# Probabilities turned whole from batch 2 on, the stack completed by transfers between SBUF rows, and other orders in the opening and in batch 0

## The chip, the cores and the metric

One core of a Trainium2 chip runs one program, a fused cross-attention and feed-forward layer over 16 batches. The metric is the device time of one execution in microseconds: 1970.97 us, the median of 3 runs (1969.54 to 1971.58).

## The reference, cut to what matters

```
x: (16, 512, 512)   ctx: (16, 77, 512)
n = layernorm(x)
Sim = n @ w1 + ctx @ w2 + (n * w3) @ ctx^T + b           # (512, 77) per batch
A = softmax(Sim over the 77)                              # "probabilities"
hq_hat = A @ ctx                                          # (512, 512)
hc_bar = softmax(max over 77 of Sim, over the 512 rows) @ n
x1 = x + [n, hq_hat, n * hq_hat, n * hc_bar] @ W_qv + b_qv
m = layernorm(x1)
h = m @ W1 + b1                                           # 2048 wide
act = relu(h + phase term of sin(theta + 0.1 h))
out = x1 + act @ W2 + b2
```

## The kernel before, in words

Every float32 product is made of three reduced-precision matmuls (`three`): each operand is split into a high part (a cast by ScalarE) and a low part (value minus high, a subtraction by VectorE), and high x high, high x low and low x high are summed in PSUM. A matmul has 128 x 128 stationary and 128 x 512 moving elements.

The context has 77 rows (J), so the products with the probabilities are packed instead (`stacked`): the high and low part of the turned probabilities and the parts of the context rows are stacked along the 128 rows that are summed, in two blocks of `at_s`. Block 0 holds the 77 rows of the high part and below them the first 51 rows (JA = 128 - 77) of the low part; block 1 holds 77 rows of the high part again and the 26 remaining rows of the low part, 103 rows in all (JB). So the turned probabilities are needed at SBUF rows other than those on which they come out of a plain turn. Compute engines keep their rows, so the kernel splits first and turns afterwards: `prob_high` (ScalarE, two copies) and `prob_low` (VectorE, two subtractions) lay out in `split_prob` what each block is to hold, `prob_turn` (TensorE) turns both blocks of each of 4 row tiles through PSUM, 8 turns, and `stack_out` (ScalarE) and `second_stack_out` (VectorE) copy the two blocks to `at_s`. `split_prob` lies in the buffer `prs`, which otherwise holds the split products n * hq_hat.

Each engine has its own written-out list of work, and semaphores join them. A stage f = 0 to 15 (FT = 16) of batch b makes one slice of 128 hidden columns: `hidden(b, f)` (12 matmuls to `hid`), on ScalarE phase and h, on VectorE the reduction of the phase, on ScalarE the sine, on VectorE the sine term, then relu and its two parts; `second(b, f)` (12 matmuls to `acc`) follows LAG = 3 stages later. In between stands the attention of the next batch, n = b + 1: the spreads (the two parts of the normalized, turned x, T) and g (the scaled context) at f = 0 to 2, `sim` at f = 3, `sim_rows` at 4, `spread_max` at 5, `prob_turn` at 8, the stack copies at 8 and 9, `hq_hat(n, 0)` at NA - 1 = 9, the attention products at NA = 10 and the second normalization at 11 to 14. SP loads x, the turned x and the context rows of the next batch (`ctx_load`) and stores the output; POOL streams the weights, whose split copies were written to DRAM during batch 0, and makes the square roots.

The opening (`attention_first` on each engine) makes ten chunks of context rows times W_qv (`rows_in`, `high_parts`, `low_part`, `multiply`, `product_add`, `product_out`), keeps them in DRAM (hqw), and does the attention of batch 0 between them. POOL issues the loads of w3, w0 and x of batch 1 there. In batch 0 (`first`) the weights are also split (`w1_high`, `w1_low`, `tile_high`, `tile_low`), which loads ScalarE and VectorE more than later batches do. `add_b2` adds the last bias to the residual, `add_first_part` and `add_last_part` add the two sums of `acc`.

## Time and profile before

| | |
|---|---|
| median of 3 runs | 1970.97 us |
| the profiled execution | 1970.5 us |
| its span in the trace | 1968.7 us |
| TensorE matmul busy | 1948.3 us, 99%, 8807 instructions |
| TensorE weight load busy | 1598.2 us, 81% |
| VectorE busy | 1387.2 us, 70% |
| ScalarE busy | 988.9 us, 50% |
| GpSimd busy | 389.4 us, 20% |
| DMA | 391.73 MB, mean 199 GB/s |

The span is the time between the first and the last instruction; the rest of the execution's time lies around it. Matmuls are pipelined, so a matmul that is shown with 390 ns follows the one before it after a shorter time; the spacing of their starts is what counts. The granted clock (PEclk) is TensorE's share of full speed, at one of two levels, 1.2 and 2.4 GHz; a value between is a mean over the stretch.

### The profile page before, as it was taken

Reading aid. Unit: us, or ns where it says so; the run is one execution under the profiler, and the core shown is the slowest. Engines: PE = TensorE matmul, PEld = TensorE weight load, DVE = VectorE, ACT = ScalarE, POOL = GpSimd, SP = SyncE. Lnnn points to the kernel's source line nnn. Section 1 sums busy time; section 2 is a strip of 40 time slices with the busy share of each in tenths; the row PEclk is TensorE's granted clock in tenths of the full one; section 3 lists DMA queues with packets and bytes.
Section 4 is the critical chain, followed back from the end, with each engine's and each line's share of the span. In section 5 each row is a group of like instructions: output and inputs, shape, how many; then the busy total and the mean of one; then the engine's idle time right before and its main releaser. Section 6 shows DMA issues by size and latency. Waiting matters only on the chain.

```text
span 1968.7 us, 24691 instructions
## 1 busy us (share of the span) xinstructions
PE 1948.3 (99%) x8807; PEld 1598.2 (81%) x8807; DVE 1387.2 (70%) x2405; ACT 988.9 (50%) x1676; POOL 389.4 (20%) x834
## 2 busy tenths in 40 slices
PE   8899999999999999999999999999999999999999
PEld 6678888888888888888888888888888888888887
DVE  6888776767777676776767767676776767767554
ACT  4574635536355363644636355363653636446343
POOL 1122212121211212112121211212112121121210
PEclk9999999999999999999999999999999999999999
DMA  8476947577474775747667485764747757476473
GB/s 247 166 266 240 291 145 224 182 212 222 152 224 144 243 220 160 237 145 222 203 189 226 138 236 166 225 221 155 232 134 242 222 166 231 146 221 181 146 216 119
DMA packets 140849, 391.73 MB, mean 199 GB/s; under 512 B 21876, under 2 KB 34856, under 8 KB 138808
## 3 DMA queue, kind: packets, MB, share of 16 engines
q0 software_dynamic: 83568, 304.29, 49.6%
q1 hardware_dynamic: 57016, 85.83, 14.0%
q8 instruction: 71, 1.16, 0.2%
q14 instruction: 50, 0.41, 0.1%
q10 hardware_dynamic: 144, 0.04, 0.0%
HBM read 351.83 MB, written 38.27 MB: 198 GB/s over the span
## 4 chain that ended last, share of the span: by engine, by line
PE 92%; DVE 3%; ACT 2%; DMA 1%; issue 1%; SPq 0%; DVEq 0%; ACTq 0%
PE acc L500 17%; PE acc L502 17%; PE acc L501 17%; PE hid L502 11%; PE hid L500 11%; PE hid L501 11%; PE mis L586 1%; PE acc L508 1%; PE acc L509 1%; PE mis L508 1%; PE mis L509 1%; PE mis L500 1%; PE mis L502 1%; PE mis L501 1%; DMA ph<-in_ctx_turned 1%
## 5 line engine op out<-in xcount | busy, mean ns | idle before, releaser
L500 PE MATMUL acc<-ws,act 128*128 128x512 f32 x1024 | 402.8, 393 | 1.7 <-DVE act L1174 1.7
L500 PE MATMUL hid<-T,w1s 128*128 128x512 f32 x1024 | 402.8, 393 | 0.4 <-ACT h L849 0.3
L502 PE MATMUL acc<-ws,act 128*128 128x512 f32 x1024 | 399.2, 390 | 0.0
L502 PE MATMUL hid<-T,w1s 128*128 128x512 f32 x1024 | 399.0, 390 | 0.0
L501 PE MATMUL acc<-ws,act 128*128 128x512 f32 x1024 | 398.7, 389 | 0.0
L501 PE MATMUL hid<-T,w1s 128*128 128x512 f32 x1024 | 398.7, 389 | 0.0
L1168 DVE TENSOR_SCALAR kk<-ph 128x512 f32<-128x512 f32 x256 | 108.8, 425 | 329.5 <-ACT ph L846 329.5
L855 ACT ACTIVATE act<-h 128x512 fp32r<-128x512 f32 x256 | 162.0, 633 | 351.7 <-DVE h L1160 330.3
L846 ACT ACTIVATE ph<-hid,hbias 128x512 f32<-128x512 f32 x256 | 175.8, 687 | 285.3 <-PE hid L502 285.0
L1509 POOL DMA_DIRECT2D ws<-w2x_dram x240 | 127.5, 532 | 556.2 <-PE acc L502 546.7
L1174 DVE SCALAR_TENSOR_TENSOR act<-h,act 128x512 fp32r<-128x512 f32 x256 | 176.0, 688 | 74.4 <-ACT act L855 73.1
L500 PEld LDWEIGHTS acc<-ws,act 128*128 128x128 f32 x1024 | 192.4, 188 | 41.7 <-DVE act L1174 2.5
L500 PEld LDWEIGHTS hid<-T,w1s 128*128 128x128 f32 x1024 | 192.3, 188 | 41.7 <-issue 1.2
L502 PEld LDWEIGHTS hid<-T,w1s 128*128 128x128 f32 x1024 | 192.2, 188 | 40.4
L502 PEld LDWEIGHTS acc<-ws,act 128*128 128x128 f32 x1024 | 192.2, 188 | 40.4
L501 PEld LDWEIGHTS acc<-ws,act 128*128 128x128 f32 x1024 | 192.4, 188 | 38.9
L501 PEld LDWEIGHTS hid<-T,w1s 128*128 128x128 f32 x1024 | 192.5, 188 | 38.7
L1503 POOL DMA_DIRECT2D w1s<-w1x_dram x240 | 129.6, 540 | 454.1 <-PE hid L502 442.1
L1160 DVE SCALAR_TENSOR_TENSOR h<-ph,camp,h 128x512 f32<-128x512 f32 x256 | 191.0, 746 | 0.0
L849 ACT ACTIVATE h<-hid,cols 128x512 f32<-128x512 f32 x256 | 174.6, 682 | 26.0 <-DVE act L1174 26.0
L1170 DVE TENSOR_TENSOR ph<-ph,kk 128x512 f32<-128x512 f32 x256 | 177.4, 693 | 8.8
L859 ACT ACTIVATE ph<-ph 128x512 f32<-128x512 f32 x256 | 158.3, 618 | 1.3 <-DVE ph L1170 1.0
(181 smaller groups left out, 2741.9 us busy)
## 6 DMA issues: line engine op xcount, KB each, us to landing
w1s<-w1x_dram POOLq DMA_DIRECT2D x240, 512.0 KB, 3.9
ws<-w2x_dram POOLq DMA_DIRECT2D x240, 512.0 KB, 4.6
ws<-wqx_dram POOLq DMA_DIRECT2D x56, 512.0 KB, 3.6
full<-in_x_turned SPq DMA_DIRECT2D x15, 1024.0 KB, 8.2
out_x<-X SPq DMA_DIRECT2D x15, 1024.0 KB, 4.7
X<-in_x SPq DMA_DIRECT2D x14, 1024.0 KB, 8.6
w_raw<-in_L_ffn_W SPq DMA_DIRECT2D x32, 256.0 KB, 3.8
w1x_dram<-w1s POOLq DMA_DIRECT2D x16, 512.0 KB, 4.0
```

The lines of the kernel that those rows point to most:

```text
L500: pe.matmul(dst, w_hi, m_hi, start=start, stop=False)
L501: pe.matmul(dst, w_hi, m_lo, start=False, stop=False)
L502: mm = pe.matmul(dst, w_lo, m_hi, start=False, stop=stop)
L846: nc.scalar.activation(ph[:, f % 2], hid[:, f % 2], ACT.Identity, bias=hbias[:, f:f + 1], scale=HSCALE).then_inc(t_done, 1)
L849: nc.scalar.activation(h2[:, f % 2], hid[:, f % 2], ACT.Identity, bias=b1c[:, f:f + 1], scale=1.0).then_inc(h2_done, 1)
L855: nc.scalar.activation(act[:, f % 4, 0], h2[:, f % 2], ACT.Relu).then_inc(act_hi, 1)
L859: nc.scalar.activation(ph[:, f % 2], ph[:, f % 2], ACT.Sin, scale=TWO_PI_BELOW).then_inc(s_done, 1)
L1160: ve.scalar_tensor_tensor(out=h2[:, f % 2], in0=ph[:, f % 2], scalar=camp[:, f:f + 1], in1=h2[:, f % 2], op0=ALU.mult, op1=ALU.add).then_i ...
L1170: ve.tensor_tensor(ph[:, f % 2], ph[:, f % 2], kk[:], ALU.subtract).then_inc(r_done, 1)
L1174: ve.scalar_tensor_tensor(out=act[:, f % 4, 1], in0=h2[:, f % 2], scalar=0.0, in1=act[:, f % 4, 0].bitcast(F32), op0=ALU.max, op1=ALU.subtract
L1503: po.dma_start(w1s[:, s].rearrange("p a c k -> p (a c k)"), w1x_dram[f % FT].rearrange("p a c k -> p (a c k)")).then_inc(w1_in[s], 16)
L1509: po.dma_start(ws[:, slot_of(p)], tile_source(p, last, w2x_dram, wqx_dram)).then_inc(w_in[slot_of(p)], 16)
```

## The change

From batch 2 on (n > 1), `whole_prob_turn` turns the unsplit probabilities at f = 6: four turns of 77 columns to rows 0 to 76 of one PSUM bank. `whole_stack_out` (ScalarE, f = 7) casts them to the high rows of block 0 and copies these to block 1. `whole_stack_low` (VectorE, f = 7) writes the low part to `at_lo`, rows 0 to 76 of a part of `prs`, and SP moves its first 51 rows to rows 77 to 127 of block 0 and the other 26 to rows 77 to 102 of block 1 (`stack_low_in`), two transfers between SBUF rows of 104 and 53 KB. `hq_hat(n, 0)` waits for them, and for `max_exponentials`, for which `prob_turn` waited before. Batches 0 and 1 keep the old way.

In the opening: `context_high(0, 0)`, `sim_bias(0)`, `row_exponentials(0)` and, on VectorE, `context_low(0, 0)`, `low_part(5)`, `low_part(6)` and `low_part(7)` change places; SP puts `product_out(2)` and `rows_in(8)` ahead of two weight loads; POOL's load of w3 waits for one low part fewer, that of w0 also for the high parts of chunk 6, and that of x for one low part more; ScalarE makes g of batch 1 at its end. In batch 0: the spreads and `g_low` of batch 1 stand at f = 0 and 1, and `add_b2` moves from f = 3 to 6 (one tile each) to f = 12 and 15 (two tiles each).

The diff, with few lines around each edit and indentation shortened:

```
@@ -133,6 +133,7 @@
...
 split_high = [split_prob[:, :, 2 * k * J:(2 * k + 1) * J] for k in range(2)]
+at_lo = prs[0:J, 1, 1]
 e_bc = sb("e_bc", [P, R])

@@ -205,7 +206,7 @@
...
 ebc_done = sem("ebc_done"); erec_done = sem("erec_done"); at_done = sem("at_done")
-split_hi = sem("split_hi"); split_lo = sem("split_lo"); at_out = sem("at_out")
+split_hi = sem("split_hi"); split_lo = sem("split_lo"); at_out = sem("at_out"); at_low = sem("at_low"); at_in = sem("at_in")
 hqh_done = sem("hqh_done"); full_done = sem("full_done")

@@ -392,6 +393,12 @@
...
         stack_load(n, hqw_raw, hqw_tail, hqw_dram, ctx_in)
+    def stack_low_in(n):
+        sp.wait_ge(at_low, n - 1)
+        sp.dma_start(at_s[J:P, 0].bitcast(F32), at_lo[0:JA].bitcast(F32)).then_inc(at_in, 16)
+        sp.dma_start(at_s[J:JB, 1].bitcast(F32), at_lo[JA:J].bitcast(F32)).then_inc(at_in, 16)

@@ -429,10 +436,10 @@
...
         rows_in(7)
+        product_out(2)
+        rows_in(8)
         first_tile_load(0)
         first_tile_load(1)
-        product_out(2)
-        rows_in(8)
         product_out(3)

@@ -471,6 +478,8 @@
...
                 continue
+            if f == NA - 3 and not first:
+                stack_low_in(n)
             if n + 1 == B:

@@ -622,6 +631,12 @@
...
+    def whole_prob_turn(n):
+        pe.wait_ge(prob_done, n + 1)
+        for t in range(RT):
+            tr = pe.transpose(mis[0:J, 1, t * P:(t + 1) * P], prob[:, t], ident[:])
+        tr.then_inc(at_done, 1)
     def prob_turn(n):

@@ -634,6 +649,9 @@
...
             pe.wait_ge(at_out, 2 * (n + 1))
+            if n > 1:
+                pe.wait_ge(ebc_done, n + 1)
+                pe.wait_ge(at_in, 32 * (n - 1))
             pe.wait_ge(hq_lo, 2 * (n + 1))

@@ -720,8 +738,10 @@
...
                 spread_max(n)
-            if f == 8 and not last:
+            if f == 8 and first:
                 prob_turn(n)
+            if f == 6 and not first and not last:
+                whole_prob_turn(n)
             if f == 3 and not last:

@@ -884,6 +904,13 @@
...
+    def whole_stack_out(n):
+        sc.wait_ge(at_done, n + 1)
+        need(sc, att_done, RT * n)
+        nc.scalar.copy(at_s[0:J, 0], mis[0:J, 1]).then_inc(at_out, 1)
+        sc.wait_ge(at_out, 2 * n + 1)
+        nc.scalar.copy(at_s[0:J, 1], at_s[0:J, 0].bitcast(F32)).then_inc(at_out, 1)
     def w0_high(n, c):

@@ -901,7 +928,6 @@
...
         g_high(0)
-        context_high(0, range(0, 1))
         high_parts(4)

@@ -910,10 +936,11 @@
...
             full_copy(0, t)
+        context_high(0, range(0, 1))
+        sim_bias(0)
         high_parts(6)
-        sim_bias(0)
+        row_exponentials(0)
         high_parts(7)
-        row_exponentials(0)
         prob_high(0)

@@ -946,20 +973,24 @@
...
         product_copy(9)
+        g_high(1)
...
             g = FT * b + f
-            if f == 1 and not last:
+            if f == 1 and not first and not last:
                 spread_high(n, 0, pn)
...
                 row_exponentials(n)
-            if f == 6 and not last:
+            if f == 6 and first:
                 prob_high(n)
+            if f == NA - 3 and not first and not last:
+                whole_stack_out(n)
+            if f == NA - 1 and first:
+                stack_out(n)
             if f == NA - 1 and not last:
-                stack_out(n)
                 w0_high(n, 0)

@@ -979,7 +1010,10 @@
...
                 continue
-            if f == 1:
+            if f == 0 and first:
+                for c in range(C):
+                    spread_high(n, c, pn)
+            if f == 1 and not first:
                 spread_high(n, 2, pn)

@@ -1214,6 +1248,10 @@
...
+    def whole_stack_low(n):
+        ve.wait_ge(at_out, 2 * n + 1)
+        low(at_lo, mis[0:J, 1], at_s[0:J, 0]).then_inc(at_low, 1)
     def second_stack_out(n):

@@ -1281,23 +1319,23 @@
...
     def add_b2(n, t):
-        ve.wait_ge(x2_done, RT * n + t + 1)
+        ve.wait_ge(x2_done if n else a_evac, RT * n + t + 1)
         if n == 0:
...
-        ve.wait_ge(xb2_done, RT * (b + 1))
+        need(ve, xb2_done if b else x2_done, RT * (b + 1))
         ve.wait_ge(ffn2_done, FT * b + NA - LAG)
...
-        if whole:
+        if whole or b == 0:
             ve.wait_ge(xb2_done, RT * (b + 1))
-        else:
+        if not whole:
             ve.wait_ge(ffn2_done, FT * (b + 1))

@@ -1320,7 +1358,6 @@
...
             norm_first(t)
-        context_low(0, range(0, 1))
         low_part(3)

@@ -1330,14 +1367,14 @@
...
         turned_low(0, 3, 0, full_done, t1_lo)
+        low_part(5)
         sim_column(0)
-        low_part(5)
         product_add(2)
+        context_low(0, range(0, 1))
         product_add(3)
-        low_part(6)
         product_add(4)
         row_max(0)
-        low_part(7)
+        low_part(6)
         probabilities(0)

@@ -1346,6 +1383,7 @@
...
         context_low(0, range(1, 2))
+        low_part(7)
         row_mean(0, range(2, C))

@@ -1393,7 +1431,7 @@
...
                 chunk_low(n, 0)
-            if f == 2 and not last:
+            if f == 2 and not first and not last:
                 g_low(n)

@@ -1406,8 +1444,10 @@
...
                 sine_term(g - 1, (f - 1) % FT)
-            if f == NA - 2 and not last:
+            if f == NA - 2 and first:
                 second_stack_out(n)
+            if f == NA - 3 and not first and not last:
+                whole_stack_low(n)
             if first and 3 <= f < 3 + CN - GAP:

@@ -1415,15 +1455,24 @@
...
                 scale(n, 1)
+            if f == 0 and first:
+                g_low(n)
+                spread_low(n, 0, pn)
+                spread_low(n, 1, pn)
             if f == 1 and not last:
                 sim_column(n)
-                spread_low(n, 0, pn)
-                spread_low(n, 1, pn)
+                if first:
+                    spread_low(n, 2, pn)
+                    spread_low(n, 3, pn)
+                else:
+                    spread_low(n, 0, pn)
+                    spread_low(n, 1, pn)
             if f == FT - 1 and n + 1 < B:
...
                 center(n + 1, 1)
-            if first and 3 <= f < 3 + RT:
-                add_b2(b, f - 3)
+            if first and f in (NA + 2, NA + 5):
+                for t in range(2 * (f - NA - 2) // 3, 2 * (f - NA - 2) // 3 + 2):
+                    add_b2(b, t)
             if not first and f in (3, 4):

@@ -1432,8 +1481,9 @@
...
                 probabilities(n)
+            if f == 6 and first:
+                prob_low(n)
             if f == 6 and not last:
-                prob_low(n)
                 row_mean_scale(n)

@@ -1575,11 +1625,12 @@
...
         po.wait_ge(s_w1q_lo, C)
-        po.wait_ge(c_tlo, 4)
+        po.wait_ge(c_tlo, 3)
         po.dma_start(w3_sb[:], wqv_dram[3]).then_inc(s_w3, 16)
         po.wait_ge(tr1, RT)
+        po.wait_ge(c_thi, GAP + 1)
         po.dma_start(w0_sb[:], wqv_dram[0]).then_inc(s_w0, 16)
-        po.wait_ge(c_tlo, GAP + 1)
+        po.wait_ge(c_tlo, GAP + 2)
         po.dma_start(X[:, 1], x_rows[1]).then_inc(x1_in, 16)
```

## Rows read from the trace of the kernel before

**Rows 1.** Windows: length, busy us by engine, granted clock, DMA share, GB/s

```profile
0.00:77.00 77.00, 67.76 (x299) 53.70 (x300) 57.34 (x123) 33.95 (x62) 12.28 (x28) 0.96 0.65 200
77.00:200.00 123.00, 115.31 (x507) 91.52 (x507) 99.56 (x173) 75.19 (x132) 27.34 (x55) 0.97 0.72 249
200.00:1840.00 1640.00, 1639.93 (x7444) 1349.39 (x7443) 1165.34 (x2006) 828.74 (x1398) 327.24 (x706) 1.00 0.64 197
```

**Rows 2.** TensorE's waits: tile, line, releaser; total us, times, longest

```profile
PE mis L500 <- DVE T L1027: 4.6, 1, 4.6
...
PE acc L500 <- DVE act L1027: 3.7, 2, 1.9
...
PE mis L615 <- ACT tmp_w L864: 1.9, 1, 1.9
```

**Rows 3.** Timeline of TensorE, `prob_turn`, one batch: start, duration, line, tiles, shapes

```profile
728.79 0.27 PE L630 MATMUL mis<-ident,prs 128*128 128x128 f32 x1
728.90 0.27 PE L631 MATMUL mis<-ident,prs 128*103 128x128 f32 x1
...
729.90 0.40 PE L501 MATMUL acc<-ws,act 128*128 128x512 f32 x1
```

**Rows 4.** Timeline of TensorE, `spread_max` of the same batch

```profile
712.00 0.60 PE L622 MATMUL mis<-ident,rmax 128*128 128x128 f32 x4
...
712.67 0.39 PE L501 MATMUL acc<-ws,act 128*128 128x512 f32 x1
```

**Rows 5.** Timeline of TensorE, `sim_rows` of the same batch

```profile
706.22 0.43 PE L615 MATMUL mis<-ident,tmp_w 77*128 77x77 f32 x4
...
706.76 0.39 PE L501 MATMUL acc<-ws,act 128*128 128x512 f32 x1
```

**Rows 6.** Timeline of VectorE, f = 5 and 7 of the same batch

```profile
715.96 0.48 DVE L1203 TENSOR_TENSOR prob<-prob,rrec 128x308 f32<-128x308 f32 x1
...
726.86 0.75 DVE L1160 SCALAR_TENSOR_TENSOR h<-ph,camp,h 128x512 f32<-128x512 f32 x1
```

**Rows 7.** Timeline of TensorE, `second` at f=6, `hq_hat(n, 0)` at f=9

```profile
717.91 0.39 PE L500 MATMUL acc<-ws,act 128*128 128x512 f32 x1
...
737.85 0.39 PE L508 MATMUL mis<-at_s,hqs 128*128 128x512 f32 x1
```

**Rows 8.** Timeline of ScalarE, f = 6 and 7 of the same batch

```profile
719.34 0.44 ACT L879 CAST prs<-prob 128x308 fp32r<-128x308 f32 x1
...
725.08 0.67 ACT L846 ACTIVATE ph<-hid,hbias 128x512 f32<-128x512 f32 x1
```

**Rows 9.** DMA issues: count, KB each, median us from issue to landing

```profile
bqv_bc<-in_L_xattn_b_qv SPq DMA_DIRECT2D x1, 256.0 KB, 6.9
...
tmp_w<-in_ctx_turned SPq DMA_DIRECT2D x16, 154.0 KB, 6.4
```

**Rows 10.** Short windows of the opening and of batch 0, columns of rows 1

```profile
18.00:20.00 2.00, 0.27 (x2) 0.25 (x2) 1.60 (x3) 1.98 (x5) 0.00 (x0) 1.00 0.17 54
...
32.00:34.00 2.00, 1.86 (x7) 1.61 (x8) 1.79 (x4) 0.09 (x1) 1.30 (x2) 0.56 1.09 369
...
82.00:83.00 1.00, 1.00 (x6) 0.84 (x5) 0.97 (x2) 0.86 (x2) 0.00 (x0) 1.00 0.68 268
```

**Rows 11.** Timeline of TensorE, similarity of batch 1 in batch 0

```profile
95.44 0.68 PE L500 MATMUL mis<-T,gs 128*77 128x512 f32 x1 [4.62 <-DVE T L1027]
...
100.57 0.40 PE L500 MATMUL acc<-ws,act 128*128 128x512 f32 x1
```

**Rows 12.** Chain that ended last, in order: start, us, what

```profile
24.59 10.70 DMA ph<-in_ctx_turned
```

**Rows 13.** Timelines of ScalarE and VectorE in batch 0

```profile
91.63 1.48 ACT L813 ACTIVATE tmp_w<-tmp_w,cols 128x77 f32<-128x77 f32 x4
...
94.01 1.28 DVE L1027 TENSOR_TENSOR T<-full,T 128x512 fp32r<-128x512 f32 x2
...
126.62 0.68 DVE L1287 TENSOR_TENSOR X<-X,b_bc 128x512 f32<-128x512 f32 x1
```

More of the change, by code:

```diff
@@ L473, in body @@
                         continue
+                    if f == NA - 3 and not first:
+                        stack_low_in(n)
                     if n + 1 == B:
@@ L623, in spread_max, with whole_prob_turn @@
                 tr.then_inc(mbc_done, 1)
+            def whole_prob_turn(n):
+                pe.wait_ge(prob_done, n + 1)
+                for t in range(RT):
+                    tr = pe.transpose(mis[0:J, 1, t * P:(t + 1) * P], prob[:, t], ident[:])
+                tr.then_inc(at_done, 1)
             def prob_turn(n):
@@ L722, in body @@
                         spread_max(n)
-                    if f == 8 and not last:
+                    if f == 8 and first:
                         prob_turn(n)
+                    if f == 6 and not first and not last:
+                        whole_prob_turn(n)
                     if f == 3 and not last:
@@ L953, in body @@
                     g = FT * b + f
-                    if f == 1 and not last:
+                    if f == 1 and not first and not last:
                         spread_high(n, 0, pn)
@@ L981, in body @@
                         continue
-                    if f == 1:
+                    if f == 0 and first:
+                        for c in range(C):
+                            spread_high(n, c, pn)
+                    if f == 1 and not first:
                         spread_high(n, 2, pn)
@@ L1395, in body @@
                         chunk_low(n, 0)
-                    if f == 2 and not last:
+                    if f == 2 and not first and not last:
                         g_low(n)
@@ L1408, in body @@
                         sine_term(g - 1, (f - 1) % FT)
-                    if f == NA - 2 and not last:
+                    if f == NA - 2 and first:
                         second_stack_out(n)
+                    if f == NA - 3 and not first and not last:
+                        whole_stack_low(n)
                     if first and 3 <= f < 3 + CN - GAP:
@@ L1424, in body @@
                         center(n + 1, 1)
-                    if first and 3 <= f < 3 + RT:
-                        add_b2(b, f - 3)
+                    if first and f in (NA + 2, NA + 5):
+                        for t in range(2 * (f - NA - 2) // 3, 2 * (f - NA - 2) // 3 + 2):
+                            add_b2(b, t)
                     if not first and f in (3, 4):
@@ L1434, in body @@
                         probabilities(n)
+                    if f == 6 and first:
+                        prob_low(n)
                     if f == 6 and not last:
-                        prob_low(n)
                         row_mean_scale(n)
```

70 lines of the change are left out of this document (50 added, 20 removed).

## The prediction

> **What bounds the kernel now.** I read first how busy each engine is in four stretches, then what TensorE waited for. From 200 to 1840 us, which is most of batches 1 to 15, TensorE is busy in 1639.93 of 1640.00 us at full granted clock, while VectorE and ScalarE have 29% and 49% to spare [rows 1]. There the time is the number of TensorE instructions times their spacing, and work taken from any other engine is worth nothing. The opening (0 to 77 us) has 9.2 us without TensorE work and batch 0 (77 to 200) has 7.7 us; the granted clock is 0.96 and 0.97 in them [rows 1], so part of their matmuls ran at the lower of the two levels. The list of TensorE's waits names where: 4.6 us once, for the low half of T before the similarity of batch 1; twice at the split context rows, the longest 1.9; 1.9 once before `sim_rows` of batch 0 [rows 2]. So there are three accounts: the steady batches, the opening, batch 0.
>
> **Account 1, the steady batches: eight turns become four.** Spacing is read from start to start. `prob_turn` begins at 728.79 and the second matmul behind it starts at 729.90 [rows 3]: 1.11 us. One matmul is in that; 23 of them start from 706.76 to 712.00 us [rows 4, 5], 0.228 us each. So eight turns take 0.88 us. `spread_max` is four turns of 128x128: 712.00 to 712.67, less one spacing, 0.44 us [rows 4]. `whole_prob_turn` issues four turns whose stationary block has 77 columns and whose moving block is the same 128x128 identity, so I price it like `spread_max`, 0.44 us. Bounds: 0.31 us, what the four 77-wide turns of `sim_rows` took by the same subtraction [rows 5], and 0.88 if nothing is won. It applies to batches 2 to 15, fourteen of them: 14 x 0.44 = 6.2 us, bounds 0 and 8.0.
>
> A rule bears on this price. The row shows that in `prob_turn` the turn with 103 stationary columns follows 0.11 us behind that with 128, and 0.88 for eight says that both take that [rows 3]; four turns with 128 stationary and 77 moving columns took only 0.31 [rows 5]. The Trainium skill, page "TensorE: Matmul & The Clock Gate", section LDWEIGHTS, says that a weight load costs its columns divided by 1.2 GHz; by that rule `sim_rows` would have been the dearer one and 77 stationary columns the cheap case. The trace goes with the moving columns, so the sum keeps 0.44; the other reading is rival 3.
>
> **Does the new stack arrive in time?** Three new waits stand on TensorE's path.
> First, `whole_prob_turn` moves from f = 8 to f = 6 and now waits for the probabilities themselves. In the batch read, VectorE finished them at 716.44, and hidden(6) gave way to the next matmuls at 717.91 [rows 6, 7]: 1.5 us to spare. A turn that waited longer than 0.44 us would eat the gain of its batch. `row_exponentials` and `probabilities` keep their places, so I cost this at nothing.
> Second, ScalarE. Its two copies of `prob_high` (0.44 and 0.45 us, from 719.34 to 720.03) go from f = 6; two copies of 77 x 512, about 0.6 us each, come at f = 7 ahead of phase(7), which started at 725.08 [rows 8]; one copy goes at f = 9. Phase(7) comes about 0.6 us later. VectorE loses the two short subtractions of `prob_low` and trades a copy of 103 x 512 for a subtraction of 77 x 512, one f earlier. Queued behind on both engines are h, relu and the low half of act; TensorE takes these three f later, and neither of its engines was late once in this stretch [rows 1, 2]. Nothing.
> Third, the DMAs. VectorE's sine term of f = 7 ended at 727.6 [rows 6]; 0.6 later by ScalarE and 0.7 for the subtraction gives 728.9. SP has nothing in its queue there (its x load of f = 6 is long out) and needs 1 us to issue two transfers. `hq_hat(n, 0)` comes at 737.85 - 0.44 = 737.4 [rows 7], 7.5 us behind the second issue. The load of the same size on SP's queue, 154 KB, took 6.4 us from issue to landing in the median of 16 [rows 9], with six others behind it; here two go alone. At 6.4 us it still fits, with 1.1 to spare. The Trainium skill, page "DMA: Bandwidth & Descriptors", in its section on the anatomy of one DMA, gives about 2.0 us fixed plus bytes at 436 GB/s, an estimate of 2.4 us for this one; no run here shows such a transfer yet. The waits for ebc_done and at_in add no instruction of the array. Account 1 stays at 6.2.
>
> **Account 2, the opening.** `sim_bias(0)` leaves its place behind `high_parts(6)`, which waited for a context load; with it go TensorE's wait of 1.9 us [rows 2] and what followed: the clock was granted at 0.56 in 32 to 34 us [rows 10], the lower level for most of it, and six matmuls ran at 0.43 us instead of 0.228, the spacing of 12 matmuls in 5.13 us that batch 0 shows [rows 11], another 1.2. Together 3.1 us. Of the 9.2 us there remain, without those 1.9 and about 3.4 of the start (some 1.5 until the identity is there, and the longer of the two waits for context rows), some 3.9: a wait of 1.8 at chunk 3 [rows 2], and smaller ones up to `hq_hat(0, 0)`. The one of 1.8 goes, since `low_part(3)` no longer stands behind `context_low`; but the turns that follow need VectorE's `turned_low`, which now stands behind `product_add(0)` and so behind the b_qv row. That landed 6.9 us after its issue [rows 9], just ahead of this addition. w3's 1 MB is now issued one context chunk sooner, into transfers that are still at work; before, it came behind an interval (18 to 20 us) with a DMA share of 0.17 [rows 10]. That fills the hole, and may hold b_qv up by 1 to 2 us. Later it pays: w3 and w0 no longer sit ahead of rows 6, 7 and the hqw stack (row load 7 took 10.7 us, and the chain that ended last ran through it [rows 12]), and `high_parts(7)` and `low_part(7)` leave the road to `hq_hat(0, 0)` in part. Of these 3.9 I count 0.4. From `hq_hat(0, 0)` to the end of the opening TensorE has no gap, but VectorE hasn't either, and `low_part(7)` now falls into that stretch (0.6 us); I count it as hidden, its cover being the 2 us between chunk products and their use. Account 2: 3.5 us; bounds 1 and 6.
>
> **Account 3, batch 0.** At f = 3 the similarity of batch 1 started at 95.44 after 4.62 us of nothing, and its 12 matmuls took until 100.57 [rows 11], 2.4 us more than at full clock. What it waited for was VectorE's low half of T, chunks 2 and 3, at 94.01, behind ScalarE's `g_high`, 1.48 us for four scalings and 0.45 for the cast, from 91.63 [rows 13]. The change takes `g_high(1)` ahead of the batch and does the four spreads one f sooner. Without it VectorE could have gone on 2.4 us earlier. Against that: ahead of the batch `g_high(1)` needs the context load, and the DMA engines were still 68% busy at 82 to 83 us [rows 10], so it will wait until near 82 and push phase(0) back by some 1.7 us (1.9 for itself, less what ScalarE had free there); and four spreads in a row put phase(1), and with it hidden(3), back by some 1.5. TensorE's one long wait becomes two or three short ones. I take 1.9 us for the earlier start, plus the 2.4 of the clock: 4.3. The clock's 0.97 over 123 us [rows 1] is 3.7 us at full level, which the 5.13 us of these matmuls and the wait ahead of them use up; so the other 3.1 us of waits in this batch, all short ones, left it at the upper level, and I expect the same of the new ones. Bounds: 0 (the new waits add up to the old one, and the clock falls all the same) and 7.0.
> `add_b2` leaves f = 3 to 6. Only the one of f = 6, 0.68 us at 126.62 [rows 13], stands in a stretch where VectorE runs without a gap and TensorE waits for act: 0.6 us gained. At f = 12 and 15 VectorE has room; nothing lost. Some of this is eaten by ScalarE's table loads at f = 5 and 6, which nothing moves. Account 3: 4.5 us, bounds 0 and 7.6.
>
> **Sum.** 6.2 + 3.5 + 4.5 = 14.2 us. The profiled execution took 1970.5 us (its span 1968.7 and 1.8 around it), 0.5 below the median of the runs. 1970.5 - 14.2 = 1956.3; against the median 1956.8. I predict 1956.5 us.
>
> **Rivals.**
> 1. Only the steady part comes. The opening is held by b_qv and batch 0 by the late context load, at 1 and 0 to 1.5 us: 1970.97 - 6.2 - 1 to 2.5, that is 1961.3 to 1963.8. For it: both new orders stand on transfers in a loaded stretch. Against: 1.9 us at `sim_rows` was a pure matter of order.
> 2. The transfers come late, and the kernel is slower. Place: `hq_hat(n, 0)` of batches 2 to 15. Every microsecond past 7.5 from the second issue costs 14 us. With 10.7 us, the longest of these loads [rows 12], the wait is 3.2 us in each batch, 45 us in all, less 14: 2002. It decides from a landing of 7.5 + 14.2/14 = 8.5 us. Against: that load had the saturated DMA of the opening.
> 3. The turns go by their stationary columns: 0.11 x 77/128 = 0.066 us each, 0.26 for four, 0.62 saved per batch, 8.7 in all: 1954.0. That is what the LDWEIGHTS rule of the Trainium skill would make of it. Rows 3 and 5 speak against.
> 4. The stack is not ready at f = 6: a wait of 0.4 us or more in each batch cancels account 1, with the rest kept: 1963.
>
> **Chances.** Forecast (1953 to 1960.5) 0.64; rival 1 0.16; rival 3, or an opening and batch 0 near their upper bounds (1950 to 1953.5), 0.10; rival 4 0.05; rival 2 0.03; other 0.02. The range is 1952 to 1963. A measurement of this kernel can tell 0.2%, about 4 us, from no change. Faster 0.95, within 0.02, slower 0.03: all but rival 2 and a piece of the rest lie below 1967.
>
> **What would show it.** TensorE's instructions fall by 56. The gap from hidden(6) to the matmul behind the turns is 0.44 plus a spacing. TensorE's busy share stays whole from 200 us on, and batches are 0.44 us shorter. No wait for at_s at `hq_hat`. `sim_rows(0)` follows without a wait; the 4.62 us row is gone, with waits of about 1 to 2 us at hidden(2), hidden(3) or the similarity in its place. The forecast is wrong if a wait for a transfer or the probabilities shows in steady batches, or the end of batch 0 (near 200 us) moves by under 5 or over 11 us.

## The result and the profile after

The changed kernel took 1960.47 us (median of 5 runs, 1960.17 to 1962.34); the kernel before took 1969.54 us beside it (5 runs, 1968.32 to 1971.58). The ratio is 0.9955, with a 95% interval of 0.9944 to 0.9965: 9 us faster, where 14.2 were forecast. 1960.5 lies inside the range given (1952 to 1963), but 4 us above the 1956.5 forecast: at the very edge of the band that had a chance of 0.64 (1953 to 1960.5), and just short of rival 1's (1961.3 to 1963.8). The profiled execution of the changed kernel took 1960.47 us, its span 1958.7; the span before was 1968.7, so the two traces have 10.0 us between them.

Windows of the changed kernel, which answer to [rows 1]:

```profile
0.00:77.00 77.00, 70.97 (x321) 55.89 (x322) 61.83 (x128) 35.69 (x65) 12.29 (x29) 1.00 0.73 221
77.00:200.00 123.00, 115.31 (x507) 92.29 (x506) 98.55 (x172) 76.06 (x133) 29.48 (x56) 0.97 0.72 249
200.00:1840.00 1640.00, 1639.11 (x7411) 1347.51 (x7410) 1159.53 (x1983) 825.34 (x1383) 329.53 (x716) 1.00 0.65 199
```

The opening has 3.2 us more of TensorE work in it and its clock is whole. Part of that clock is chance: in e4, e6 and e7 below, whose opening is the same code, it was 0.50 from 8 to 10 us (0.59 in the kernel before), and their openings take 69.0 to 69.3 us all the same. The second row has the same TensorE time and the same clock, 115.31 us and 0.97, as before: nothing was won there. TensorE's waits, which answer to [rows 2]:

```profile
PE hid L509 <- ACT h L869: 4.0, 1, 4.0
PE acc L509 <- DVE act L1208: 2.3, 2, 1.6
PE mis L595 <- DVE T L1061: 1.7, 1, 1.7
PE acc L509 <- DVE act L1061: 1.7, 1, 1.7
...
PE acc L509 <- DVE X L1304: 0.7, 1, 0.7
```

The wait of 4.6 us for the low half of T is gone, and one of 4.0 us for ScalarE's h stands in its place. The wait of 1.9 us for `tmp_w` at `sim_rows` of the opening is gone too. The wait of 1.7 us for T stands in the opening, at 21.13; before, the same place had 0.61. The last row is new.

The first of the eight turns of `xin`, the normalized rows of the second normalization, divides the execution into stages. It stands just ahead of f = 15, so what a batch does at f = 15 counts to the next stage here. Before, then after (start, duration):

```profile
73.97 1.03 PE L586 MATMUL mis<-ident,xin 128*128 128x128 f32 x8
...
189.46 1.04 PE L586 MATMUL mis<-ident,xin 128*128 128x128 f32 x8
...
308.89 1.04 PE L586 MATMUL mis<-ident,xin 128*128 128x128 f32 x8
```

```profile
69.24 1.03 PE L595 MATMUL mis<-ident,xin 128*128 128x128 f32 x8
...
184.83 1.04 PE L595 MATMUL mis<-ident,xin 128*128 128x128 f32 x8
...
304.95 1.03 PE L595 MATMUL mis<-ident,xin 128*128 128x128 f32 x8
```

Differences of these starts, and of the last one to the span's end, give this table. The runs of the next section are in it too.

| kernel | opening, to the first turn | batch 0 | batch 1 | rest | span |
|---|---|---|---|---|---|
| before | 73.97 | 115.49 | 119.43 | 1659.8 | 1968.7 |
| changed | 69.24 | 115.59 | 120.12 | 1653.8 | 1958.7 |
| e1, steady part alone | 73.18 | 114.79 | 118.92 | 1653.7 | 1960.6 |
| e2, batch 0 as before | 69.35 | 115.65 | 118.94 | 1653.8 | 1957.7 |
| e3, add_b2 as before | 70.73 | 116.36 | 118.96 | 1653.8 | 1959.8 |
| e4, stores late | 69.14 | 111.62 | 120.17 | 1653.7 | 1954.6 |
| e5, g_high(1) at f=1 | 72.10 | 111.39 | 120.14 | 1653.8 | 1957.4 |
| e6, stores late, spreads split | 69.33 | 111.36 | 119.76 | 1653.8 | 1954.2 |
| e7, stack late | 69.04 | 115.34 | 124.58 | 1669.2 | 1978.2 |
| e8, POOL's loads as before | 70.97 | 115.35 | 120.11 | 1653.7 | 1960.1 |
| e9, b_qv early | 69.14 | 111.81 | 118.94 | 1653.7 | 1953.6 |
| e10, turned_low first | 69.99 | 111.15 | 118.93 | 1653.7 | 1953.8 |

The 10.0 us are: opening -4.73, batch 0 +0.10, batch 1 +0.69, rest -6.06. The last column but one repeats to 0.1 us wherever the stack is the same, so a single trace tells there. The first doesn't: the opening of one and the same code moves by over a microsecond (e3 against the changed kernel). Batch 0 moves too: before, e1 and e2 have the same code there and take 115.49, 114.79 and 115.65. All three stand idle for 4.6 us ahead of the similarity, but behind it the clock was back for the last matmuls of the 12 in e1, and not in the other two. Batch 1 repeats to 0.05 us (118.92 to 118.96) where nothing is late in it.

**Steady batches.** The new turns in one steady batch of the changed kernel, with the matmuls behind them:

```profile
712.58 0.60 PE L637 MATMUL mis<-ident,prob 128*77 128x128 f32 x4
...
713.25 0.39 PE L510 MATMUL acc<-ws,act 128*128 128x512 f32 x1
```

712.58 to 713.25 less one spacing of 0.228 is 0.44 us, what `spread_max` takes [rows 4]. The stack on its way, in the order of its engines: VectorE's probabilities, ScalarE's copies, VectorE's low part, SP's issues, and the reader.

```profile
710.63 0.48 DVE L1237 TENSOR_TENSOR prob<-prob,rrec 128x308 f32<-128x308 f32 x1
```

```profile
719.05 0.56 ACT L910 CAST at_s<-mis 77x512 fp32r<-77x512 f32 x1
719.65 0.62 ACT L912 CAST at_s<-at_s 77x512 fp32r<-77x512 f32 x1
```

```profile
722.62 0.68 DVE L1061 TENSOR_TENSOR prs<-mis,at_s 77x512 fp32r<-77x512 f32 x1
```

```profile
723.32 0.74 SPq L400 DMA_DIRECT2D at_s<-prs  x1
724.11 0.80 SPq L401 DMA_DIRECT2D at_s<-prs  x1
```

```profile
732.09 0.39 PE L517 MATMUL mis<-at_s,hqs 128*128 128x512 f32 x1
```

The probabilities are ready 1.5 us ahead of their turn, as worked out; the reader comes 8.0 us behind the second issue and has no wait in brackets.

**Batch 0.** ScalarE and TensorE of the changed kernel (in brackets the idle time before, and what ended it):

```profile
80.86 1.48 ACT L833 ACTIVATE tmp_w<-tmp_w,cols 128x77 f32<-128x77 f32 x4 [5.92 <-DMA ctx_raw<-hqw_dram]
82.36 0.45 ACT L836 CAST gs<-tmp_w 128x308 fp32r<-128x308 f32 x1
82.72 0.68 ACT L866 ACTIVATE ph<-hid,hbias 128x512 f32<-128x512 f32 x1
```

```profile
84.12 0.77 PE L509 MATMUL hid<-T,w1s 128*128 128x512 f32 x1 [4.05 <-ACT h L869]
...
89.33 0.39 PE L509 MATMUL hid<-T,w1s 128*128 128x512 f32 x1
```

```profile
78.00:79.00 1.00, 1.00 (x6) 0.81 (x5) 1.00 (x1) 0.00 (x0) 0.00 (x0) 1.00 0.37 145
79.00:80.00 1.00, 1.00 (x5) 0.56 (x3) 0.05 (x1) 0.00 (x0) 0.00 (x0) 1.00 0.20 78
80.00:81.00 1.00, 0.07 (x1) 0.00 (x0) 0.00 (x0) 0.14 (x1) 0.00 (x0) 1.00 0.19 59
...
83.00:84.00 1.00, 0.00 (x0) 0.00 (x0) 0.54 (x2) 1.00 (x3) 0.00 (x0) 0.50 0.00 0
```

`g_high(1)` waited 5.92 us for the context rows of batch 1, with phase(0) and so hidden(2) behind it. Behind those 4.05 us the granted clock was 0.50, the lower level, and the 12 matmuls of hidden(2) took 5.21 us (84.12 to 89.33), 2.5 more than at full clock. The old pair, a long wait and 12 slow matmuls [rows 11], stands 11 us earlier and has nearly its old size. How late phase(0) was shows against the same row of the kernel before:

```profile
82.14 0.69 ACT L846 ACTIVATE ph<-hid,hbias 128x512 f32<-128x512 f32 x1 [2.48 <-PE hid L502]
```

Counted from the first turn of `xin`, phase(0) came at 8.17 us before and at 13.48 in the changed kernel: 5.3 us later.

### The profile page after: what moved, and what is told of

Same layout as the page of the kernel before. It is cut to its first block, busy times and chain, and to the rows that moved or that the text cites. A ratio compares the mean times of both kernels' runs of the same rounds, so it can differ in the third digit from the quotient of the medians.

```text
span 1958.7 us, 24566 instructions
## 1 busy us (share of the span) xinstructions
PE 1940.7 (99%) x8751; PEld 1591.0 (81%) x8751; DVE 1378.9 (70%) x2377; ACT 985.6 (50%) x1662; POOL 388.9 (20%) x834
## 3 DMA queue, kind: packets, MB, share of 16 engines
q8 instruction: 71, 1.16, 0.2%
## 4 chain that ended last, share of the span: by engine, by line
PE 92%; DVE 3%; ACT 2%; issue 1%; DMA 1%; SPq 1%; DVEq 0%; ACTq 0%
PE acc L509 17%; PE acc L511 17%; PE acc L510 17%; PE hid L509 11%; PE hid L511 11%; PE hid L510 11%; PE mis L595 1%; PE acc L517 1%; PE acc L518 1%; PE mis L517 1%; PE mis L518 1%; PE mis L511 1%; PE mis L509 1%; PE mis L510 1%; DMA ctx_raw<-hqw_dram 0%
```

## The experiments

**e1: the new stack alone.** Opening, batch 0 and add_b2 are as in the kernel before; only this is kept:

```diff
+            if f == 6 and not first and not last:
+                whole_prob_turn(n)
+            if f == NA - 3 and not first and not last:
+                whole_stack_out(n)      # ScalarE; whole_stack_low(n) on VectorE
+            if f == NA - 3 and not first:
+                stack_low_in(n)         # SP
```

> Theory: the three accounts add up, and the steady batches alone are worth 14 x 0.44 = 6.1 us: 0.9969 of the kernel before. Rival: the turns are worth more (0.62 per batch, 8.7 us, 0.9956), and the order of the opening and of batch 0 then brought next to nothing.

Measured: 1963.97 us (7 runs, 1962.32 to 1965.55), 1970.33 beside it; ratio 0.9971, 0.9959 to 0.9982. Its last stage has the 1653.7 of the changed kernel. The medians are 6.4 us apart. Account 1 is shown to stand by itself.

**e2: batch 0 as before,** with the new opening and the new stack; all four spreads and `g_high(1)` at f = 1, add_b2 at f = 3 to 6.

```diff
-                g_high(1)
...
-                        for c in range(C):
-                            spread_high(n, c, pn)
...
-                    if first and f in (NA + 2, NA + 5):
+                    if first and 3 <= f < 3 + RT:
+                        add_b2(b, f - 3)
```

> New opening and new stack, but the order of batch 0 (T, g and add_b2) as before. Theory: batch 0's new order is worth nothing or less, so this is as fast as the changed kernel or up to 1 us faster, 4.7 + 6.1 = 10.8 us below the kernel before (0.9945); TensorE waits 4.6 us before the similarity of batch 1. Rival: the new order does bring some of the 4.5 us forecast and something else lost it: then this is 3 to 5 us slower than the changed kernel (0.997).

Measured: 1959.46 us (5 runs, 1958.24 to 1960.04); ratio 0.9945, 0.9933 to 0.9958. The old order of batch 0 is back, with its old wait, and the kernel is 1 us faster than the changed one:

```profile
90.83 0.68 PE L509 MATMUL mis<-T,gs 128*77 128x512 f32 x1 [4.59 <-DVE T L1057]
```

Batch 0 takes 115.65 us against 115.59: the edits of account 3 are worth nothing in batch 0, and batch 1 pays 1.18 for them. Against e1, whose batch 0 is the same code, this run isolates the opening: 3.83 us between the first columns of the two traces, 4.5 between the medians.

**e3: add_b2 alone as before,** everything else as changed.

```diff
-                    if first and f in (NA + 2, NA + 5):
-                        for t in range(2 * (f - NA - 2) // 3, 2 * (f - NA - 2) // 3 + 2):
-                            add_b2(b, t)
+                    if first and 3 <= f < 3 + RT:
+                        add_b2(b, f - 3)
```

> The changed kernel with add_b2 at f = 3 to 6 again. Theory: the additions at f = 15 hold VectorE up into batch 1 and cost about 1.1 us there; back in their old place that wait (0.7 us on add_last_part at f = 3 of batch 1) is gone and the kernel is 0.5 to 1.1 us faster than the changed one. Rival: they helped in batch 0 by 0.6 us, and this is 0.6 us slower.

Measured: 1961.28 us (5 runs, 1960.19 to 1961.57); ratio 0.9954, 0.9942 to 0.9967. As a time this is a miss: it came out no faster. The stages tell why. Batch 1 is 1.16 us shorter than in the changed kernel, batch 0 is 0.77 longer, and the opening, which has no edit, took 1.5 us more in this trace. Of the 0.77, 0.62 lie between the similarity of batch 1 and the wait for act behind it (34.14 us here, 33.52 in the changed kernel), with slow stretches of equal length ahead: about the 0.6 that the prediction gave the new places of add_b2.

The 1.5 us of the opening can be read from this trace:

```profile
21.04 1.22 PE L595 MATMUL mis<-ident,w_sb 128*128 128x128 f32 x8 [2.32 <-DVE T L1061]
...
23.07 0.63 PE L509 MATMUL acc<-T,act 128*128 128x512 f32 x1
23.50 0.63 PE L510 MATMUL acc<-T,act 128*128 128x512 f32 x1
...
26.44 0.39 PE L509 MATMUL mis<-T,gs 128*77 128x512 f32 x1
```

VectorE had T ready at the same time as in the changed kernel (the turns start at 21.04 and 21.13), but TensorE was through with its earlier work sooner and stood idle for 2.32 us instead of 1.72. Behind that the granted clock fell, to 0.62 in 22 to 24 us and 0.53 in 24 to 26, and matmuls started 0.43 us apart; in the changed kernel it was 1.00 in both windows. The first matmul of the similarity of batch 0 starts at 26.44 instead of 24.92, 1.5 us later, which is the whole difference of the two openings (70.73 and 69.24).

What happens in batch 1, by VectorE of the changed kernel:

```profile
200.46 1.28 DVE L1325 TENSOR_TENSOR X<-X,b_bc 128x512 f32<-128x512 f32 x2
...
219.51 2.47 DVE L1304 TENSOR_TENSOR X<-X,acc 128x512 f32<-128x512 f32 x4
```

The pair of add_b2 at f = 15 puts all of VectorE's later work 1.2 us back: the four last additions of batch 0's output start 34.7 us behind batch 1's first turn, 33.5 in e2 (218.49 less 185.00), and TensorE waits 0.73 us for them at 220.34.

**e4: POOL's w1x stores behind the context loads.**

```diff
                     if first and f == 0:
+                        po.wait_ge(ctx_in, ctx_count(1))
                         for k in range(3):
                             w1_store(k)
```

> The changed kernel, but POOL's first three weight stores of batch 0 wait until the context of batch 1 has landed. Theory: g_high(1) waits for a context load that shares the DMA engines with these stores; without them it lands 3 us or more sooner, TensorE's 4.05 us wait at hidden(2) shrinks below 1 us, the clock stays at its upper level, and the kernel is 4 to 6 us faster than the changed one. Rival: the wait comes from ScalarE's own work (g_high and four spreads in a row): then at most 1 us, and the wait stays near 3 to 4 us.

Measured: 1956.93 us (5 runs, 1956.45 to 1957.95); ratio 0.9934, 0.9922 to 0.9947. The expectation was 4 to 6 us: it is 3.5 between the medians and 4.1 between the spans, so at or just under its lower end. The wait at hidden(2) is down to 0.2 us at most, below 1 as expected; the row of 1.51 is hidden(3), behind the four spreads in a row, for which the prediction had 1.5. The cause in batch 0 is confirmed:

```profile
76.71 1.49 ACT L833 ACTIVATE tmp_w<-tmp_w,cols 128x77 f32<-128x77 f32 x4 [1.87 <-DMA ctx_raw<-hqw_dram]
78.23 0.45 ACT L836 CAST gs<-tmp_w 128x308 fp32r<-128x308 f32 x1
78.59 0.69 ACT L866 ACTIVATE ph<-hid,hbias 128x512 f32<-128x512 f32 x1
```

```profile
84.50 0.47 PE L509 MATMUL hid<-T,w1s 128*128 128x512 f32 x1 [1.51 <-ACT h L869]
88.38 0.43 PE L509 MATMUL mis<-T,gs 128*77 128x512 f32 x1 [0.90 <-DVE T L1061]
```

```profile
77.00:200.00 123.00, 117.22 (x524) 93.73 (x523) 102.43 (x179) 77.13 (x135) 32.59 (x62) 1.00 0.77 266
```

The context rows are there 4.15 us sooner: 1.7 us because SP's last issue for them ends at 70.85 instead of 72.54, and the rest because they land 5.9 us behind it instead of 8.3. The other traces agree: 6.2 to 6.4 us in e6, e9 and e10, which hold the stores back too, and 8.4 to 8.6 in e3, e7 and e8, which don't. Waits of 1.5 and 0.9 us are left, the clock stays at its upper level, and batch 0 is 3.97 us shorter.

**e5: g_high(1) at f = 1, the stores as changed.** The other way to the same end: the scaling stands behind h(1), where the rows have long landed.

```diff
-                g_high(1)
...
                     phase_and_hidden(b, f)
+                    if first and f == 1:
+                        spread_high(n, 2, pn)
+                        spread_high(n, 3, pn)
+                        g_high(n)
```

> The changed kernel with g_high(1) at f = 1, behind h(1) and the last two spreads, instead of ahead of the batch; the first two spreads at f = 0; the weight stores untouched. Theory: phase(0) no longer stands behind the context load (which lands near 81 us all the same), so the 4.05 us wait at hidden(2) and the low clock go; waits of about 0.6 us at hidden(3) and 0.8 before the similarity stay: 4 to 5 us faster than the changed kernel, 1956. Rival: g_high, 1.9 us of ScalarE, is the load wherever it stands, and the similarity waits for g 3 us or more: at most 1.5 us gained.

Measured: 1956.45 us (5 runs, 1956.15 to 1959.18), 1970.09 beside it; ratio 0.9932, 0.9918 to 0.9945. Batch 0 takes 111.39 us with waits of 0.30 and 0.31 where e4 has 1.5 and 0.9:

```profile
85.98 0.47 PE L509 MATMUL hid<-T,w1s 128*128 128x512 f32 x1 [0.30 <-ACT h L869]
89.30 0.46 PE L509 MATMUL mis<-T,gs 128*77 128x512 f32 x1 [0.31 <-DVE gs L1064]
```

1.8 us less of waits, but only 0.2 us less of batch 0: new waits of 0.82 and 0.25 us stand at 98.75 and 105.02. VectorE and ScalarE seem to set the pace of this stretch. Between the medians it is 4.0 us faster than the changed kernel, the lower end of what was expected. The trace is that of the slowest execution (1959.18), 2.7 us above the median, with an opening of 72.10: b_qv landed late, TensorE stood idle for 3.30 us ahead of 22.46, and the clock was 0.88, 0.50 and 0.77 in the 6 us behind.

**e6: three repairs together.** Stores late as in e4, `g_high(1)` where the change has it, the last two spreads behind h(1), and the second pair of add_b2 at f = 13 instead of 15.

```diff
                     if first and f == 0:
+                        po.wait_ge(ctx_in, ctx_count(1))
...
-                        for c in range(C):
-                            spread_high(n, c, pn)
+                        spread_high(n, 0, pn)
+                        spread_high(n, 1, pn)
...
+                    if first and f == 1:
+                        spread_high(n, 2, pn)
+                        spread_high(n, 3, pn)
...
-                    if first and f in (NA + 2, NA + 5):
+                    if first and f in (NA + 2, NA + 3):
```

> Three cures together on the changed kernel: POOL's first stores behind the context load, the last two spreads behind h(1) with their low parts ahead of w1_low(4), and the second pair of add_b2 at f = 13 instead of 15. Theory: 3.5 to 4.1 us by the stores, the waits of 1.5 (hidden(3)) and 0.9 us (similarity) nearly gone, and the 0.8 us wait in batch 1 gone with 1.1 us: 6 to 7 us faster than the changed kernel, about 1954. Rival: TensorE then meets VectorE and ScalarE sooner in f = 5 to 9 of batch 0, where they run without a gap, and half of it is lost there: 1957.

Measured: 1955.96 us (5 runs, 1954.82 to 1957.35); ratio 0.9929, 0.9916 to 0.9941. Expected were 6 to 7 us, measured are 4.5 below the changed kernel, between the theory and its rival. Batch 0 is 111.36, so splitting the spreads adds only 0.3 us to the late stores. Batch 1 is 119.76 here and 118.94 in e9 and e10, which have the same code there; in e6 VectorE waited for a context load:

```profile
207.69 0.69 DVE L1189 CUSTOM_DVE_ANT_0 e_bc<-ctx_raw,w_bc 77x512 f32<-77x512 f32 x1 [2.34 <-DMA ctx_raw<-hqw_dram]
```

**e7: the low part of the stack one f later.**

```diff
-                    if f == NA - 3 and not first and not last:
+                    if f == NA - 2 and not first and not last:
                         whole_stack_low(n)
```

> The changed kernel with the low part of the stack one f later (f = 8), so that the second transfer is issued about 1.4 us before hq_hat can begin. This measures how long the transfers take. Theory, with 2.0 to 2.6 us from the last issue to the count: TensorE waits about 1 us in each of 14 batches, 14 to 20 us slower than the changed kernel. Rival, with 6.4 us like the context load of that size: 5 us each, 70 us slower. If nothing is late, the transfers take under 1.4 us.

Measured: 1980.25 us (4 runs, 1978.09 to 1981.41); ratio 1.0050, 1.0036 to 1.0064: slower than the kernel before. Its waits, SP's issues in one batch, and the reader:

```profile
PE mis L517 <- DMA at_s<-prs: 14.9, 14, 2.6
```

```profile
735.89 0.74 SPq L400 DMA_DIRECT2D at_s<-prs  x1
736.68 0.80 SPq L401 DMA_DIRECT2D at_s<-prs  x1
```

```profile
740.64 0.47 PE L517 MATMUL mis<-at_s,hqs 128*128 128x512 f32 x1 [1.06 <-DMA at_s<-prs]
```

The reader waited for the transfers and starts 4.0 us behind the start of the second issue. Over the batches it is 3.5 to 4.2 us in thirteen of them and 5.4 in the first, whose second issue starts at 254.38:

```profile
259.76 0.47 PE L517 MATMUL mis<-at_s,hqs 128*128 128x512 f32 x1 [2.59 <-DMA at_s<-prs]
```

So the landing that the prediction took at 6.4 us takes 3.5 to 5.4, and in the changed kernel, where 7.9 to 8.0 are there, at least 2.5 us are to spare. Rival 2 was a real mechanism with the wrong landing time: 14 waits in series, 14.9 us of them, cost 19.5 us of span as soon as they exist, at the upper end of the 14 to 20 expected. Behind the longest, 2.59 us, the clock fell again (0.65 and 0.50 from 260 to 264 us), and batch 1 is 4.5 us longer.

**e8: POOL's loads of w3, w0 and x at their old waits,** the rest as changed.

```diff
-                po.wait_ge(c_tlo, 3)
+                po.wait_ge(c_tlo, 4)
...
-                po.wait_ge(c_thi, GAP + 1)
...
-                po.wait_ge(c_tlo, GAP + 2)
+                po.wait_ge(c_tlo, GAP + 1)
```

> The changed kernel with POOL's loads of w3, w0 and x at their old places. Theory: they put 1 to 2 MB ahead of the context rows and the hqw stack; prob_high (behind high_parts(7)) and hq_hat(0, 0) come 1 to 3 us later, and the opening's 4.7 us fall to 2 to 3.5. Rival: the order on ScalarE and VectorE alone made the opening's gain, and this is as fast as the changed kernel.

Measured: 1961.74 us (4 runs, 1961.43 to 1961.95); ratio 0.9957, 0.9943 to 0.9971. ScalarE's row and then TensorE's:

```profile
33.90 0.62 ACT L813 CAST act<-ph 128x512 fp32r<-128x512 f32 x1 [2.44 <-DMA ph<-in_ctx_turned]
```

```profile
36.03 0.30 PE L645 MATMUL mis<-ident,prs 128*128 128x128 f32 x1 [1.82 <-DVE prs L1061]
```

POOL issues w0 at 22.74 instead of 29.68 (w3 at 17.80 instead of 14.57), it shares the DMA engines with a context chunk, and that chunk stands ahead of `prob_high(0)` on ScalarE. The opening is 1.73 us longer; the clock was whole, and the 1.82 us that TensorE waits at 36.03, where the changed kernel has no such wait, account for it. The medians are 1.3 us apart. Of the opening's 4.7 us 3.0 are left, as expected. In the prediction this was the clause "Later it pays"; it pays about that much. Which of the three loads does it isn't separated: w0 is issued earlier than in the changed kernel, w3 later.

**e9 and e10: what still holds the opening.** Both are e6 with one move. e9 issues b_qv ahead of context rows 3; e10 takes the first turned_low ahead of product_add(0).

```diff
+                sp.dma_start(bqv_bc[:], row(b_qv, P)).then_inc(s_bqv, 16)
                 rows_in(3)
```

```diff
-                product_add(0)
                 low_part(4)
                 turned_low(0, 0, 0, full_done, t1_lo)
+                product_add(0)
                 turned_low(0, 1, 0, full_done, t1_lo)
```

> The kernel of the sixth run, with SP's load of b_qv issued ahead of context rows 3, so some 4 us sooner (8.4 instead of 12.4). Theory: what still holds the opening is that VectorE stands at product_add(0) for b_qv until 19.1 us, with turned_low queued behind it; b_qv now lands near 15.5, product_add(0) starts behind g_low near 17.2, turned_low near 18.8, and TensorE's wait of 1.7 us at 21.2 shrinks to 0.3 to 0.7. The opening's end (first turns of xin, 69.3) comes 1.0 to 1.4 us sooner; in all about 1954.8 against the 1955.96 of the sixth run. Rival: the context loads that it is put ahead of land later by as much, the wait moves to them, and nothing is won (1956) or up to 1 us is lost.

> The kernel of the sixth run, with low_part(4) and the first turned_low moved ahead of product_add(0) in VectorE's order; b_qv's load stays where it is. Theory (VectorE's order at b_qv is the cause): turned_low(0,0) starts near 18.7 instead of 20.3, so the wait of 1.7 us at 21.2 goes to about 0.3; the second turned_low stands behind product_add(0) at 19.1 and comes near 19.8 instead of 20.9. Gain 1.0 to 1.4 us, 1954.8. Rival: the turn of the next chunk then waits instead, and the product of rows 0 goes out no sooner; the chain through row loads 5 to 7 sets the end of the opening, and it stays at 69.3 (1956).

Measured: e9 1955.75 us (5 runs, 1954.92 to 1957.02), ratio 0.9929, 0.9915 to 0.9943; e10 1955.61 us (5 runs, 1955.21 to 1957.20), ratio 0.9928, 0.9916 to 0.9941; 1969.59 beside both. Both are misses of size. The wait did shrink, from 1.69 us in e6 to 0.83 + 0.35 and 0.15 + 0.57:

```profile
20.67 0.63 PE L595 MATMUL mis<-ident,w_sb 128*128 128x128 f32 x4 [0.83 <-DVE T L1064]
21.64 0.63 PE L595 MATMUL mis<-ident,w_sb 128*128 128x128 f32 x4 [0.35 <-DVE T L1064]
```

Counted from the first turn of `w_sb` (17.43 and 18.17; 17.10 in e6), the opening takes 51.7 and 51.8 us against 52.2: 0.4 to 0.5 us gained of the 1.0 to 1.4 expected, and no more than the medians' spread. These two and e6 have the lowest medians, but the three differ by less than the runs of each, so none of them is shown to be the fastest. All three are faster than the changed kernel, by 4.5 to 4.9 us.

## Why the prediction was right in two accounts and wrong in one

**Account 1 (6.2 us) was right.** Measured are 6.06 us behind batch 1's end, and 0.51 in batch 1 with the new stack alone (119.43 to 118.92), 6.6 together. Four turns take 0.44 us, 56 instructions are gone (8807 to 8751), and no steady batch has a wait. The value from `spread_max` held, and with it the reading that these turns go by their moving columns: rival 3, the division of stationary columns by 1.2 GHz of the Trainium skill's page "TensorE: Matmul & The Clock Gate", section LDWEIGHTS, would have shown 0.26 us and doesn't. Rival 4 fell by the 1.5 us that the probabilities had to spare. Rival 2 fell by a landing of 3.5 to 5.4 us (e7). The estimate from the page "DMA: Bandwidth & Descriptors" of the Trainium skill, its section on the anatomy of one DMA, was 2.4 us; that section gives its figures for transfers issued by GpSimd, and these two are issued by SP. What e7 measured is longer, 2.7 to 3.3 us even from the end of the second issue in thirteen batches, and the measurement decides.

**Account 2 (3.5 us) was right in kind and low:** 4.73 between the traces, 3.8 to 4.5 by e1 and e2. `sim_rows(0)` follows without a wait, the clock in 0 to 77 us went from 0.96 to 1.00 (the part of it from 8 to 12 us by chance), and b_qv landed 6.7 us behind its issue (12.41 to 19.1), as the row of before said. The term that was too small is "Of these 3.9 I count 0.4". By the waits of the two traces it came to 1.5: the 1.73 at chunk 3, the 0.58 at `prob_turn` and 0.25 of the first wait for context rows went, and the wait for T at the turns grew from 0.61 to 1.72. e8 puts the moved loads alone at 1.7. I had weighed the hole they fill in the opening's DMA traffic against b_qv, and gave too little for the chunks which they no longer hold up. One part is less sure than it looks: the 1.73 at chunk 3 was only 0.33 in e1, with the same order.

**Account 3 (4.5 us) failed:** -0.1 us in batch 0, and 1.2 lost in batch 1 (the 0.69 of the table, where the stack alone had brought 0.51). Three of its steps were wrong.
1. "It will wait until near 82 and push phase(0) back by some 1.7 us." It was pushed back by 5.3 us; with the repair of e4, by 1.3. I read the landing of the context load in the clock of the kernel before, by the second in which the DMA share was 0.68 [rows 10]. A share isn't a landing: in the changed kernel the share is down to 0.2 for two microseconds before the load is in, at 80.86. And the new opening had moved all of TensorE's work 4.7 us forward, so that "near 82" on the old time axis would have had to be 77.3 on the new one; the load came 3.6 us behind that. The load's issue did move with account 2 (its last part from 75.86 to 71.65), but the rows were in only 8.3 us behind the end of that issue (72.54). With POOL's 512 KB stores held back (e4) it was 5.9 us, from 70.85 to 76.71.
2. "I expect the same of the new ones", the clock at its upper level through the new waits. That was argued for waits of 1 to 2 us. One of 4.05 came, and the clock fell; with 1.51 and 0.90 (e4) it didn't. The price of 2.4 us for the slow stretch was right (2.5), it was only paid again.
3. "At f = 12 and 15 VectorE has room; nothing lost." The change's pair at f = 15 costs 1.2 us in batch 1. The 0.6 gained by leaving the old places did come, by e3, in the distance and not in the wait: the wait for act near 126 us is 1.62 us in the changed kernel and 1.63 in e3, where it was 0.96 before.

That growth has one cause with e5's small gain. From the similarity of batch 1 to the end of that wait the distance is 33.52 us in the changed kernel (92.49 to 126.01) and 33.53 in e4 (88.38 to 121.91), whatever came before. TensorE doesn't set it, since it waits at the end; nor is VectorE busy without a gap, since it stands idle for ScalarE's phase 3.24 us ahead of 111.31 and 2.07 ahead of 119.65, while ScalarE waits for VectorE in other places. The two of them, each at times waiting for the other, seem to set the time; no run takes that chain apart. Of what TensorE wins ahead of it some 0.7 us (0.96 to 1.62) comes back as a wait. The rest of batch 0's 4 us is kept. With the repair of e4 account 3 would have given 3.9 us (115.49 to 111.62), close to the 4.5; the order of work was worth its price, only the load wasn't there.

So of the 4.2 us by which the sum was too high (14.2 against 10.0), account 1 gave 0.4 more and account 2 1.2 more, batch 0 4.6 less, and batch 1 1.2 less. That 1960.5 still lies in the range is in part luck: 1.6 us of errors one way stand against 5.8 the other. Of the signs given, those of the steady batches and of the instruction count hold. Those of batch 0 don't: a wait of 4.05 us stands where 1 to 2 were expected. And the end of batch 0 was to move by 5 us or more; the first turn of `xin` there moved by 4.63 (189.46 to 184.83), which the prediction itself had named as a sign of being wrong. Rival 1 was half true: batch 0 was held by the late context load. In the opening b_qv did cost something, since VectorE waited 1.92 us for it and TensorE's wait behind grew by 1.1, but the opening still gained 4.7 us and not 1.

Why the opening of one code takes 69.2 in one execution and 70.7 or 72.1 in another can be read from the traces. In e5 b_qv landed 1.3 us later than in the changed kernel (VectorE's wait for it was 3.26 us and ended at 20.42), and the clock fell behind TensorE's idle time of 3.30 us. In e3 b_qv was in at 19.0 as in the changed kernel, but TensorE had come to the place sooner, and the clock fell behind 2.32 us. So the place behind b_qv costs more than its wait as soon as the clock falls there, and the changed kernel's trace, with 1.72 us, is a favourable one. What stays open is why TensorE comes there sooner or later, and why the slow stretch is shorter at some times than at others behind idle times of nearly one length (12 matmuls behind 4.62 us in the kernel before, 7 or 8 in e1).

## What to carry to other kernels

When one part of a change moves the clock of everything behind it, the landings that a later part relies on have to be worked out again from their issue, not read off the old time axis. Before an instruction that waits for a load is put at the head of an engine's queue, list what else is issued in the same microseconds, stores of another queue first: holding back three stores by one wait was worth 4 us here, some 40% of what the whole change brought. And stages should be compared by an instruction that starts each of them, since a median hides a gain in one batch behind a loss in the next.

## What the runs showed of the hardware

- Two transfers between SBUF rows, 51 x 512 and 26 x 512 elements (77 x 512 together), alone on SP's queue, were usable 3.5 to 4.2 us behind the start of the second issue in thirteen batches and 5.4 in one, each issue holding SP for 0.74 to 0.85 us (e7). A load of the same volume had taken 6.4 us in the median from HBM with others behind it [rows 9].
- Small context loads on SP's queue landed 8.3 to 8.6 us behind the end of their last issue with three 512 KB stores of POOL issued beside them (changed kernel, e3, e7, e8), and 5.9 to 6.4 with these held back (e4, e6, e9, e10).
- DMA share is a poor sign of when a load is in: 0.37, 0.20 and 0.19 in the last three microseconds before a landing that held up ScalarE and, through it, TensorE.
- The granted clock was 0.50 behind an idle time of 4.05 us, and stayed there for all of the next 12 matmuls (5.21 us); behind 1.51 and 0.90 us (e4) it stayed whole. At one place of the opening it stayed whole behind 1.72 us (changed kernel) and fell behind 2.32 (e3: 0.62 and 0.53 in the next two windows of 2 us) and 3.30 (e5).
